# Pair products of a recommendation model: three sets of features, two copied as blocks within SBUF

## What is computed

```python
features = jnp.concatenate([bot_out[:, None, :], gathered], axis=1)
Z = jnp.einsum('bnd,bmd->bnm', features, features)
interact = Z[:, LI, LJ]          # pairs i > j
x = jnp.concatenate([bot_out, interact], axis=1)
return _mlp(x, [tw0, ...], [tb0, ...])   # 479 -> 1024 -> 1024 -> 512 -> 256 -> 1, relu
```

## Time and profile before

| | |
|---|---|
| median of 3 runs | 213.04 us (211.81 to 213.62) |
| span of the profiled execution | 179.6 us |
| busy in the span: TensorE matmul | 167.0 us (93%) |
| GpSimd | 100.7 us (56%) |
| VectorE, ScalarE | 82.2 us, 66.3 us |
| DMA | 19.93 MB, mean 111 GB/s |

### The profile page before, as it was taken

One profiled execution on the slowest core, in us unless ns is written; L12 is line 12 of the kernel. 1 busy time (PEld: TensorE's weight loads), 2 busy tenths in 40 slices (PEclk: granted clock), 3 DMA queues, 4 the chain that ended last, 5 costly groups with the idle time before them and its releaser, 6 DMA issues.

```text
span 179.6 us, 3315 instructions
## 1 busy us (share of the span) xinstructions
PE 167.0 (93%) x1354; PEld 128.6 (72%) x1354; DVE 82.2 (46%) x177; ACT 66.3 (37%) x103; POOL 100.7 (56%) x112
## 2 busy tenths in 40 slices
PE   1999999899599994999999999989999999999993
PEld 1335557568377783798878889977888898788992
DVE  3202588955165756374452346343506625411422
ACT  0576748664143655133033253112504611110211
POOL 3777776777777777777777777767772000000000
PEclk9999999999999999799999999999999999999999
DMA  4999972434499733242232244422223120000000
GB/s 97 369 337 391 390 239 58 100 66 89 89 302 374 285 79 86 54 100 68 44 61 51 52 105 85 93 46 62 46 59 72 24 53 7 4 0 0 0 0 4
DMA packets 10124, 19.93 MB, mean 111 GB/s; under 512 B 5639, under 2 KB 5771, under 8 KB 9981
## 3 DMA queue, kind: packets, MB, share of 16 engines
q1 hardware_dynamic: 6636, 12.89, 22.0%
q0 software_dynamic: 3328, 6.82, 16.7%
q10 hardware_dynamic: 144, 0.00, 0.0%
HBM read 18.26 MB, written 1.44 MB: 110 GB/s over the span
## 4 chain that ended last, share of the span: by engine, by line
PE 71%; DMA 10%; POOL 8%; issue 4%; SPq 2%; DVE 2%; ACT 2%; POOLq 0%; DVEq 0%; ACTq 0%
PE acc L799 14%; PE acc L803 13%; PE acc L800 12%; POOL rows L420 8%; PE feat L781 6%; PE turned L944 5%; PE feat L763 5%; DMA rows<-in_emb,index 3%; PE turned L881 3%; DMA pairs<-pair_scratch 3%; DMA pair_scratch<-dots 3%; PE acc L829 2%; PE acc L938 2%; PE feat L938 2%; DMA v<-in_bw 1%
## 5 line engine op out<-in xcount | busy, mean ns | idle before, releaser
L420 POOL DMA_INDIRECT rows<-in_emb,index x104 | 99.5, 957 | 34.4 <-issue 30.0
L799 PE MATMUL acc<-w1h,y_split 128*128 128x512 f32 x64 | 27.9, 436 | 0.0
L803 PE MATMUL acc<-w1h,y_split 128*128 128x512 f32 x64 | 26.1, 407 | 0.0
L800 PE MATMUL acc<-w1l,y_split 128*128 128x512 f32 x64 | 25.5, 399 | 0.0
L444 ACT COPY featT<-feat 128x512 f32<-128x512 f32 x16 | 17.6, 1097 | 14.4 <-PE feat L763 14.3
L457 ACT ACTIVATE y_split<-turned 128x512 fp32r<-128x512 f32 x16 | 9.7, 606 | 35.1 <-PE turned L881 35.1
L651 DVE SCALAR_TENSOR_TENSOR y_split<-turned,y_split 128x512 fp32r<-128x512 f32 x16 | 11.1, 692 | 18.7 <-ACT y_split L457 18.7
L799 PE MATMUL acc<-w2h,y_split 128*128 128x256 f32 x64 | 18.8, 294 | 0.0
L803 PE MATMUL acc<-w2h,y_split 128*128 128x256 f32 x64 | 18.0, 281 | 0.0
L763 PE MATMUL feat<-ident,rows 128*128 128x128 f32 x104 | 15.3, 277 | 2.7 <-DMA rows<-in_emb,index 2.7
L800 PE MATMUL acc<-w2l,y_split 128*128 128x256 f32 x64 | 17.8, 279 | 0.0
(11 more groups left out here) (107 smaller groups left out, 255.6 us busy)
## 6 DMA issues: line engine op xcount, KB each, us to landing
w1r<-in_w SPq DMA_DIRECT2D x8, 512.0 KB, 13.8
w2r<-in_w SPq DMA_DIRECT2D x4, 512.0 KB, 6.0
rows<-in_emb,index POOLq DMA_INDIRECT x104, 3.0
w0r<-in_w_pairs SPq DMA_DIRECT2D x3, 512.0 KB, 7.8
top<-in_top_rows SPq DMA_DIRECT2D x1, 1024.0 KB, 12.1
pair_scratch<-dots SPq DMA_DIRECT2D x8, 104.0 KB, 2.3
pair_scratch<-dots SPq DMA_DIRECT2D x8, 71.5 KB
v<-in_bw SPq DMA_DIRECT2D x1, 512.0 KB, 3.6
```

The lines of the kernel that those rows point to most:

```text
L420: pool.indirect_dma_start(rows[:, i, :], None, table, bass.IndirectOffsetOnAxis(ap=index[:, c, i:i + 1], axis=0)).then_inc(s_gather[LOTS * ...
L799: nc.tensor.matmul(dst, ah, wh, start=first, stop=False)
L800: nc.tensor.matmul(dst, ah, wl, start=False, stop=False)
L803: return nc.tensor.matmul(dst, al, wh, start=False, stop=end)
```

## The change

The 27 features become sets of 11, 11 and 5. **Tile 0** is all products of set 1 with set 0: an 11 x 11 block, copied from `dots` to `pairs` in one DMA within SBUF. ScalarE issues it, right behind its own copies and after a wait for VectorE's. **Tile 1** is the products of the last five features with all others and among themselves (110 + 16 rows), two DMAs within SBUF, issued by SyncE. **Tile 2** is the pairs inside set 0 and inside set 1 (110 rows and the bias row); it still goes through the scratch, now two writes of 11 x 10 x 64 and two reads. Pairs that occur twice have a weight of zero at one place. `dots` has 27 columns in place of 26. TensorE's layer 0 is now: tile 0 into half 0, `turn2`, tile 0 into half 1, layer 3 of the chunk before, tile 1 and tile 2 into half 0, tile 1 into half 1, `turn(0, c, 0)`, layer 4, tile 2 into half 1. ScalarE and VectorE do the second half of chunk c - 1's layer 2 output ahead of tile 1. `keep_going` does 8 matmuls in place of 11.

```diff
-        dots = sb("dots", [P, COLS, HALF])
+        dots = sb("dots", [P, FEATS, HALF])
...
-            return dots[HALF * h:HALF * h + FEATS, :, at:at + GROUPS], block_[:, q * FEATS:q * FEATS + COLS, :]
+            return dots[HALF * h:HALF * h + FEATS, :, at:at + GROUPS], block_[:, q * FEATS:(q + 1) * FEATS, :]
+        def products(h, n0, ns, m0, ms):
+            return dots[HALF * h + n0:HALF * h + n0 + ns, m0:m0 + ms, :]
+        def pair_rows(h, i, row, n):
+            return pairs[row:row + n, i, h * HALF:(h + 1) * HALF]
+        def across_out(eng, c, h):
+            eng.wait_ge(s_za, HALVES * c + h + 1)
+            eng.wait_ge(s_zd, HALVES * c + h + 1)
+            after(eng, s_xlp, PAIR_TILES * c)
+            eng.dma_start(pair_rows(h, 0, 0, PAIR_ROWS[0]), products(h, SET, SET, 0, SET)).then_inc(s_pin[h][0], 16)
...
             def pairs_back(c, h):
                 sp.wait_ge(s_za, HALVES * c + h + 1)
                 sp.wait_ge(s_zd, HALVES * c + h + 1)
+                after(sp, s_pin[h][2], PINS[2] * c)
+                for t in range(2):
+                    sp.dma_start(scratch[h, t], products(h, t * SET, SET, t * SET, SET_COLS)).then_inc(s_scr[h], 16)
                 after(sp, s_xlp, PAIR_TILES * c)
                 if (c, h) == (0, 0):
                     sp.wait_ge(s_one, 1)
+                both = 2 * SET * LAST
+                sp.dma_start(pair_rows(h, 1, 0, both), products(h, 0, 2 * SET, 2 * SET, LAST)).then_inc(s_pin[h][1], 16)
+                sp.dma_start(pair_rows(h, 1, both, PAIR_ROWS[1] - both),
+                             products(h, 2 * SET, LAST - 1, 2 * SET + 1, LAST - 1)).then_inc(s_pin[h][1], 16)
+                sp.wait_ge(s_scr[h], 32 * (c + 1))
+                base = h * 2 * SET * SET_COLS
+                main = 2 * SET_COLS * HOPS
+                sp.dma_start(pair_rows(h, 2, 0, main),
+                             flat(scratch, (base + 1) * HALF,
+                                  [[SET * HALF, 2 * SET_COLS], [HALF, HOPS], [1, HALF]])).then_inc(s_pin[h][2], 16)
+                sp.dma_start(pair_rows(h, 2, main, 2 * HOPS),
+                             flat(scratch, (base + SET_COLS * SET_COLS + HOPS) * HALF,
+                                  [[SET * SET_COLS * HALF, 2], [HALF, HOPS], [1, HALF]])).then_inc(s_pin[h][2], 16)
...
                 nc.scalar.copy(*dot_quadrant(h, 1)).then_inc(s_za, 1)
+                across_out(act, c, h)
...
                 pairs_hi(c, 0)
-                pairs_hi(c, 1)
                 if c > 0:
                     layer2_out(c - 1, 1)
+                pairs_hi(c, 1)
                 pairs_hi(c, 2)
...
                     layer2_lo(c - 1, 0)
+                    layer2_lo(c - 1, 1)
                 pairs_lo(c, 1)
                 pairs_lo(c, 2)
-                if c > 0:
-                    layer2_lo(c - 1, 1)
                 copy_out(0, c, 0)
...
-            keep_going(turned[0], 11)
+            keep_going(turned[0], 8)
...
                 layer0(c, 0, 0)
                 if c > 0:
                     turn2(c - 1, 1)
+                layer0(c, 1, 0)
+                if c > 0:
+                    layer3(c - 1)
                 layer0(c, 0, 1)
                 layer0(c, 0, 2, end=True)
-                if c > 0:
-                    layer3(c - 1)
-                layer0(c, 1, 0)
                 layer0(c, 1, 1)
                 turn(0, c, 0)
                 if c > 0:
                     layer4(c - 1)
                 layer0(c, 1, 2, end=True)
```

More of the change, by code:

```diff
@@ L40 @@
 BANK_GROUPS = GROUPS // BANKS
-HOPS = (FEATS - 1) // 2
+SET = 11
+LAST = FEATS - 2 * SET
+HOPS = (SET - 1) // 2
+SET_COLS = SET - 1
 PAIR_TILES = 3
[L43 to L46, removed]
+PAIR_ROWS = [SET * SET, 2 * SET * LAST + (LAST - 1) * (LAST - 1), 2 * SET * HOPS]
+TILE_ROWS = [PAIR_ROWS[0], PAIR_ROWS[1], PAIR_ROWS[2] + 1]
+PINS = [16, 32, 32]
 B0, B1, B2 = 512, 256, 128
@@ L55, in pair_order, with within @@
 def pair_order():
[L61 to L72, removed]
+    def within(base, flat):
+        return base + flat // SET_COLS, base + flat % SET_COLS
+    across = [(SET + n, m) for n in range(SET) for m in range(SET)]
+    last = [(n, 2 * SET + m) for n in range(2 * SET) for m in range(LAST)]
+    last += [(2 * SET + n, 2 * SET + 1 + m) for n in range(LAST - 1) for m in range(LAST - 1)]
+    inside = [within(base, n * SET + 1 + h) for base in (0, SET) for n in range(SET_COLS) for h in range(HOPS)]
+    inside += [within(base, SET_COLS * SET_COLS + HOPS + h) for base in (0, SET) for h in range(HOPS)]
+    return [across, last, inside]
 def pair_weights(w, bias):
     out = np.zeros((PAIR_TILES, P, w.shape[1]), w.dtype)
-    for at, (a, b) in enumerate(pair_order()):
-        out[at // PAIR_ROWS, at % PAIR_ROWS] = w[DIM + a * (a - 1) // 2 + b]
-    out[PAIR_TILES - 1, PAIR_ROWS] = bias
+    placed = set()
+    for i, rows in enumerate(pair_order()):
+        for row, (n, m) in enumerate(rows):
+            a, b = max(n, m), min(n, m)
+            if a != b and (a, b) not in placed:
+                placed.add((a, b))
+                out[i, row] = w[DIM + a * (a - 1) // 2 + b]
+    assert len(placed) == FEATS * (FEATS - 1) // 2
+    out[PAIR_TILES - 1, PAIR_ROWS[PAIR_TILES - 1]] = bias
     return out
@@ L200, in rec_kernel @@
         s_z, s_za, s_zd = map(sem, ("dots_done", "dots_copied_act", "dots_copied_dve"))
-        s_scr0 = [sem(f"scratch{h}_first_written") for h in range(HALVES)]
-        s_scr1 = [sem(f"scratch{h}_rest_written") for h in range(HALVES)]
+        s_scr = [sem(f"scratch{h}_written") for h in range(HALVES)]
         s_pin = [[sem(f"half{h}_pairs{i}_in") for i in range(PAIR_TILES)] for h in range(HALVES)]
@@ L285, in _, with pairs_back @@
                 load_piece(n)
-            def scratch_out(c, h):
+            def pairs_back(c, h):
                 sp.wait_ge(s_za, HALVES * c + h + 1)
                 sp.wait_ge(s_zd, HALVES * c + h + 1)
[L290 to L302, removed]
+                after(sp, s_pin[h][2], PINS[2] * c)
+                for t in range(2):
+                    sp.dma_start(scratch[h, t], products(h, t * SET, SET, t * SET, SET_COLS)).then_inc(s_scr[h], 16)
                 after(sp, s_xlp, PAIR_TILES * c)
@@ L323, in _ @@
                 for h in range(HALVES):
-                    scratch_out(c, h)
                     pairs_back(c, h)
@@ L446, in dots_out @@
             def dots_out(c, h):
-                after(act, s_scr0[h], 16 * c)
-                after(act, s_scr1[h], 16 * c)
+                dots_free(act, c, h)
                 act.wait_ge(s_z, HALVES * c + h + 1)
@@ L461, in pairs_hi @@
                 for h in range(HALVES):
-                    act.wait_ge(s_pin[h][i], (16 if i < PAIR_TILES - 1 else 32) * (c + 1))
+                    act.wait_ge(s_pin[h][i], PINS[i] * (c + 1))
                 after(act, s_l[0], 2 * c)
-                nc.scalar.copy(xh[0:PAIR_ROWS + 1, i, :], pairs[0:PAIR_ROWS + 1, i, :]).then_inc(s_xhp, 1)
+                nc.scalar.copy(xh[0:TILE_ROWS[i], i, :], pairs[0:TILE_ROWS[i], i, :]).then_inc(s_xhp, 1)
             def layer2_out(c, half):
@@ L616, in dots_out @@
             def dots_out(c, h):
-                after(dve, s_scr0[h], 16 * c)
-                after(dve, s_scr1[h], 16 * c)
+                dots_free(dve, c, h)
                 dve.wait_ge(s_z, HALVES * c + h + 1)
@@ L625, in pairs_lo @@
                 dve.wait_ge(s_xhp, PAIR_TILES * c + i + 1)
-                nc.vector.tensor_tensor(xl[0:PAIR_ROWS + 1, i, :], pairs[0:PAIR_ROWS + 1, i, :],
-                                        xh[0:PAIR_ROWS + 1, i, :].bitcast(F32), ALU.subtract).then_inc(s_xlp, 1)
+                n = TILE_ROWS[i]
+                nc.vector.tensor_tensor(xl[0:n, i, :], pairs[0:n, i, :], xh[0:n, i, :].bitcast(F32),
+                                        ALU.subtract).then_inc(s_xlp, 1)
             def copy_out(layer, c, half):
@@ L1083 @@
         aps[name] = nc.dram_tensor(name, a.shape, mybir.dt.from_np(a.dtype), kind="ExternalInput").ap()
-    scratch = nc.dram_tensor("pair_scratch", (HALVES, FEATS, COLS, HALF), F32, kind="Internal").ap()
+    scratch = nc.dram_tensor("pair_scratch", (HALVES, 2, SET, SET_COLS, HALF), F32, kind="Internal").ap()
     out = nc.dram_tensor("out_y", (BATCH, 1), F32, kind="ExternalOutput").ap()
```

16 lines of the change are left out of this document (5 added, 11 removed).

## The result

The changed kernel took **220.6 us** (median of 4 runs, 218.57 to 222.08) beside 212.49 us (211.81 to 213.62) for the kernel before in the same comparison: ratio 1.033, interval 1.027 to 1.039. The prediction was 216.2, at most 218.0. The direction was right and the size was not: 8.1 us were lost where 3.2 were forecast. Medians here are over all executions of a set, ratios and intervals leave out those over 1.5% above the kernel's fastest, so the two can differ by about a per cent.

The account below looks back on a forecast made before the run. TensorE was taken to bound mid-chunk, with GpSimd's gathers nearly as full. Terms 0 + 0.38 - 0.09 + 0.38 + 2 x (0.90 + 0.2) + 0.1 + 0.2 = 3.2 us, on 213.04: 216.2 us, own range 214.8 to 217.3, extended to 213.6 to 218.0.

Parts of the forecast that it names:

- the last one of the sum: Whole kernel: 3.2 us on a span of 179.6, time around it unchanged, added to the median 213.04, giving 216.2 us.
- Held gathers: GpSimd, chunks 1 and 2: gather i = 3 starts 1.91 us later, S (tile 0's first product) + 5.54; 0.90 + 0.2 each.
- the forecast wait for rows: TensorE, last lot of chunks 1 and 2: rows asked for at S + 22.82, landing at S + 23.72, 0.90 us.
- Turn: TensorE, chunks 1 to 3: `turn(0, c, 0)` waits 0.6 us; layer 1 0.38 later; chunk 2 -0.09, its old wait gone.
- Order in sum: New order of layer 0, chunks 1 to 3: later layer 1 plus late gathers, 2.9 us slower.
- Pair path: Copies within SBUF taken at 2.3 us; ScalarE's issue of 0.78 us costs 0.1 into chunk 2, 0.2 into chunk 3.
- the gain in chunk 0: Chunk 0: layer 1 starts 1.6 us sooner, then TensorE waits 1.6 us more ahead of the lots; gain 0.
- Clock: Rival, chance 0.08: more idle at row waits and new waits in chunks 1 and 2 bring one more low-clock stretch, 217.9 us.
- Late gathers absorbed: Rival, chance 0.14: twelve gathers behind the held one make up 1.5 us, so TensorE sees no delay; 214.0 us.
- The first gain: Rival, chance 0.06: chunk 0's 1.6 us survives, with at most 1.7 of clock, if rows come 2.5 us sooner; 210.7 us.
- Range: Whole kernel: 214.8 to 217.3 us, from landings (2 x -0.7, 2 x +0.4) and run to run scatter of some 0.5.

Follow-up runs that it names:

- second run: The changed kernel without the gathers of chunks 2 and 3 (these multiply chunk 1's rows again), repeated: 199.65 us beside 214.16 for the kernel before.

## Why the prediction was wrong, and where it was right

**The step that failed is the last one of the sum**: "The span's time around it is unchanged, so on the median of 213.04". A term of 3.2 us read from a trace of 179.6 was put on a time 33 us longer, and those 33 us were taken for something outside the span. They were inside it: 17.6 us of idle time of TensorE between small products, a clock that falls behind it, and waits that the view puts down to "remote". Moving gathers moves these, and a profile at 181 has no row of it. The rest follows from that.

- **Held gathers.** The place, the delay (S + 5.54) and the sign were right. At 181 the price was 0.87 and 0.81 us, forecast 0.9 + 0.2 each. At the upper level the forecast wait for rows is not there at all: in chunks 1 and 2 none of the four traces of the changed kernel has one. What costs there is another mechanism: three gathers that begin beside the small products in place of two, 6.4 to 8.0 us in one stretch and 4.4 to 8.0 in the next, 5.2 us together, and 5.5 us came back when the hold was taken away. This term was sized at 2.2; that the sign held at this level is in part luck.
- **Turn.** Forecast the turn at S + 5.89 and layer 1 0.38 us later than before; measured S + 5.95 and 0.47 (7.26 - 6.79), at both levels. `layer3_out`'s first instruction ended a little sooner than forecast (S + 5.80, forecast 5.86), but the turn starts 0.15 us behind it, for which the sum had 0.03.
- **Order in sum.** Forecast 0.38 - 0.09 + 0.38 + 2.2 = 2.9 us; at 181 measured 2.0 and 2.5, at 212 to 214 4.3 (by the medians).
- **Pair path.** Tile 0 takes 2.5 us from ScalarE's issue to its high part in chunk 0 (2.3 forecast), the issue 0.84 us (0.78 forecast):

```profile
52.77 0.84 ACTq L286 DMA_DIRECT2D pairs<-dots  x1
...
55.30 0.30 ACT L476 CAST xh<-pairs 121x128 fp32r<-121x128 f32 x1 [0.60 <-issue]
...
57.21 0.30 ACT L476 CAST xh<-pairs 126x128 fp32r<-126x128 f32 x1 [1.61 <-issue]
...
58.12 0.30 ACT L476 CAST xh<-pairs 111x128 fp32r<-111x128 f32 x1 [0.62 <-issue]
```

  Forecast +0.3 us outside chunk 0; at 181 measured +0.3 and -0.2 (0.999 and 1.000). That the gain in chunk 0 does not last was right. At the upper level the path costs 0.7% (0.1 to 1.4), which was not in the sum, and where is not known. The traces with it have one gap that is longer: in chunk 0 VectorE takes up the result of layer 0 late, TensorE's last product of it having started at 59.05,

```profile
63.40 0.69 DVE L654 COPY y_evac<-acc 128x512 f32<-128x512 f32 x1 [4.65 <-remote]
...
64.15 1.11 PE L892 MATMUL turned<-ident,y_evac 128*128 128x128 f32 x4 [4.01 <-DVE y_evac L654]
```

  4.4 us of TensorE's time ahead of that turn. All nine traces at the upper level with the new pair path have such a gap, 3.8 to 8.0 us, in the old order too (5.2, ahead of layer 1); the two without it have 1.9 and 2.5. While it lasts the DMA engines move 312 GB/s (window 59.7 to 64.1 of the result's trace). The gap goes with the pair path; what VectorE waits for there was not found, and SyncE's weight loads, which the new path lets start sooner, are only a guess. It does not account for the 0.7%, as far as one trace each can tell: with the path in the old order chunk 0's layer 0 starts 2.4 us sooner (54.81 against 57.17), the gap uses that up, and chunk 1 starts at 102.47, in the kernel before at 102.38.
- **Clock.** A rival asked for one more low stretch, 1.7 us. In the result's profile the mean clock is 0.915, and each long stretch of small products has half speed behind it. It was not the waits for rows that the rival named, but idle time of the same kind. The Trainium skill, "TensorE: Matmul & The Clock Gate", "What's actually happening", describes the low level as what is there unless activity lifts it; here it fell to 0.50 at the end of stretches in which TensorE stood still for most of the time (busy 1.46 of 4.60 us above), and with the gathers left out (second run) the windows of those products have 1.00: the trace agrees.
- **The other rivals.** Late gathers absorbed: at 181 they were not, 0.8 us of row wait appeared in both chunks; at the upper level no wait for rows is left, but the same delay cost more by the small products. The first gain was not kept at either level.
- **Range.** Its ends, 214.8 and 217.3, are not the plain sum of what was named for them, which would be 214.3 and 217.5; 220.6 lies outside either way. Neither end had anything for the 33 us.

**What stays open.** Why an execution is at one level or the other, and through what gathers stop TensorE. There are no records of a wait at these gaps. Executions at the upper level have only half as many records of semaphore updates (1,611 beside 3,263 for the kernel before, the same instructions in both), so one candidate is that the recording of events is what TensorE waits for when many short instructions and many descriptors are recorded at once; another is a path that instructions, semaphores and gather descriptors share. No run separates them, and every time here is of a recorded execution.

## What to carry to other kernels

Ahead of a sum, set the span of the profile beside the time of the runs that it is to be added to: here an execution's span lay some 2 us under its time, so a difference of 33 meant that the profile was of another condition and that the missing time had no row in it. Ask what that time could be made of, and widen the range by what a change moves into it. And in moving a product on the busiest engine, look at what its semaphores hold on the others: here a 1.9 us later start of a gather cost 0.8 to 0.9 us by its rows at one level, and 1.6 and 3.6 us at the other by what it came to lie beside.

## What the hardware showed that was not expected

- 64 products of 128x59 by 128x54 take 1.8 us at full pace and 2.2 to 8.8 us with gathers beside them, in executions of the upper level only; with the gathers left out 1.80. The last 40 of an 8 us stretch ran at a clock of 0.50 in the result's trace. From tile 0's first product to layer 1 it takes 6.8 us at both levels in the kernel before (82.32 to 89.11, 102.38 to 109.16), so the long products show nothing of it there.
- The same kernel on the same chip took 181.4 us in one set of runs and 214.4 in another.
- A copy within SBUF of 121 rows of 256 bytes took 0.84 us to issue on ScalarE and some 2.5 us until its reader started, no less than a write to the scratch in HBM.
